# Expert layers: the clamp of a block's last two hidden chunks, moved from VectorE to GpSimd

## What is computed

```python
def _expert(x, g, b, W1, b1, W2, b2, Wo, bo):
    x = _layernorm(x, g, b)
    x1 = x @ W1 + b1
    x2 = jnp.clip(x @ W2 + b2, -20.0, 20.0)
    hidden = jnp.clip(x1 * (x2 * jax.nn.sigmoid(x2)), -10000.0, 10000.0)
    return jnp.clip(hidden @ Wo + bo, -10000.0, 10000.0)
...
logits = xf @ router_w
scores, idx = jax.lax.top_k(logits, 2)
gate = jax.nn.softmax(scores, axis=-1)
```

## Time and profile before

| | |
|---|---|
| median of 3 runs | 2541.86 us (2539.79 to 2549.73) |
| profiled execution, its own time | 2537.98 us |
| its span, first to last instruction | 2536.1 us |
| first expert pass, first to last `product` | 280.5 to 485.3 us |
| second expert pass, first to last `product` | 2296.7 to 2505.5 us |
| busy over the span: PE, DVE, ACT, POOL | 2306.2, 2218.5, 1652.6, 1483.1 us |
| back clamp L1791 on DVE, both passes | 80 times, 32.8 us |
| front clamp L1741 on POOL, both passes | 80 times, 44.9 us |
| scatter L1732 on POOL, both passes | 142 times, 143.2 us |

### The profile page before, as it was taken

How to read it: one execution, slowest core, us unless ns; L and a number is a source line. 1 busy time by engine, 2 the same in 40 slices (tenths; PEclk the granted TensorE clock), 3 DMA queues, 4 the chain that set the end, 5 groups by cost and what they waited for, 6 DMA issues and landing times. The chain is left out here.

```text
span 2536.1 us, 44098 instructions
## 1 busy us (share of the span) xinstructions
PE 2306.2 (91%) x14954; PEld 1766.5 (70%) x14954; DVE 2218.5 (87%) x4734; ACT 1652.6 (65%) x2883; POOL 1483.1 (58%) x1075
## 2 busy tenths in 40 slices
PE   6996699658999999999999999999999999968995
PEld 3553588536777777777777777777777777747884
DVE  6766588779999999999999999999999999956886
ACT  2464244347777777787778778788778877743443
POOL 1145344326666666667668766676876766663442
PEclk8997799869999999999999999999999999988997
DMA  8821566654534454344322333223342233006665
GB/s 206 221 64 46 161 210 215 174 132 108 126 84 97 98 128 99 84 101 110 84 62 71 87 81 88 62 62 79 86 100 62 62 79 86 15 27 196 202 212 180
DMA packets 169648, 281.89 MB, mean 111 GB/s; under 512 B 32940, under 2 KB 122930, under 8 KB 169424
## 3 DMA queue, kind: packets, MB, share of 16 engines
q1 hardware_dynamic: 160208, 260.11, 40.6%
q0 software_dynamic: 9216, 18.96, 2.1%
HBM read 118.94 MB, written 62.39 MB: 72 GB/s over the span
## 5 line engine op out<-in xcount | busy, mean ns | idle before, releaser
L2438 POOL TENSOR_TENSOR b_prob<-b_prob,b_weight 128x1024 f32<-128x1024 f32 x512 | 958.7, 1905 | 505.5 <-DVE b_weight L2396 504.3
L2366 DVE TENSOR_REDUCE b_bmax<-b_score 128x16 f32<-128x1024 f32 x512 | 620.5, 1212 | 44.8 <-PE b_score L2217 29.3
L2318 ACT ACTIVATE b_prob<-b_score,b_neg_m 128x1024 f32<-128x1024 f32 x512 | 581.4, 1136 | 76.9 <-DVE b_neg_m L2374 75.1
L2353 DVE TENSOR_REDUCE b_bsum<-b_prob 128x16 f32<-128x1024 f32 x512 | 605.5, 1202 | 0.0
L2303 ACT ACTIVATE b_pT<-b_turn 128x512 f32<-128x512 f32 x1024 | 560.4, 609 | 63.4 <-PE b_turn L2230 55.2
L2230 PE MATMUL b_turn<-ident,b_prob 128*128 128x128 f32 x4096 | 532.1, 273 | 3.7 <-ACT b_pT L2303 3.6
L2230 PEld LDWEIGHTS b_turn<-ident,b_prob 128*128 128x128 f32 x4096 | 477.7, 140 | 75.7 <-ACT b_pT L2303 3.9
L2217 PE MATMUL b_score<-b_KH,b_QS 128*128 128x512 f32 x1024 | 478.8, 468 | 16.8 <-ACT b_prob L2318 14.6
L2197 PE MATMUL b_acc<-b_pT,b_V 128*64 128x256 f32 x4096 | 470.3, 382 | 0.0
L2217 PE MATMUL b_score<-b_KL,b_QS 128*128 128x512 f32 x1024 | 405.6, 396 | 0.0
L2197 PEld LDWEIGHTS b_acc<-b_pT,b_V 128*64 128x64 f32 x4096 | 282.7, 137 | 150.7 <-issue 21.4
(11 more groups left out here) (329 smaller groups left out, 2956.6 us busy)
## 6 DMA issues: line engine op xcount, KB each, us to landing
f_e_w<-f_weights SPq DMA_DIRECT2D x80, 776.0 KB
f_sorted<-zeros SPq DMA_DIRECT2D x172, 193.5 KB, 5.4
b_KH<-b_k_high SPq DMA_DIRECT2D x128, 256.0 KB
b_KL<-b_k_low SPq DMA_DIRECT2D x128, 256.0 KB
b_QS<-b_q_high SPq DMA_DIRECT2D x64, 256.0 KB, 3.8
b_QS<-b_q_low SPq DMA_DIRECT2D x64, 256.0 KB, 4.9
b_hb<-b_hT SPq DMA_DIRECT2D x31, 512.0 KB
f_e_z<-f_sorted SPq DMA_DIRECT2D x62, 129.0 KB
```

What stands on the lines that cost most here:

```text
L2318: act.activation(prob[r % 4][k][:], score[k % 2][:], ACT.Exp, bias=neg_m[r % 2][:, k:k + 1]).then_inc(prob_ready, 1)
L2353: dve.tensor_reduce(bsum[r % 2][:, k, :], prob[r % 4][k][:].rearrange("p (n c) -> p n c", c=KV_BLOCK), AX, ALU.add).then_inc(sum_ready, 1)
L2366: maxima = chain.mark(dve.tensor_reduce(bmax[r % 2][:, k, :], score[k % 2][:].rearrange("p (n c) -> p n c", c=KV_BLOCK), AX, ALU.max))
L2438: pool.tensor_tensor(tile, tile, weight[r % 2][:, k, :].unsqueeze(2).to_broadcast([P, NB, KV_BLOCK]), ALU.mult).then_inc(scaled, 1)
```

## The change

GpSimd makes the clamp of chunks 2 and 3, behind its store of block t - 2, after a wait for all four products of block t. VectorE's `clamp_back` goes, with its two waits. Since another engine now reads `hid[1]`, VectorE waits for `back_ready` of block t - 1 before product 2 of block t. What is clamped, and the semaphore that tells it, stay the same.

```diff
@@ gpsimd @@
                     if t >= 2:
                         store(t - 2)
+                    pool.wait_ge(x1_taken, chunks_before + HC * t + HC)
+                    pool.tensor_scalar(hT[t % DEEP][:, 2:HC, 0:rows_of[t]], hid[1][:, :, 0:rows_of[t]], CLAMP, -CLAMP, ALU.min, ALU.max).then_inc(back_ready, 1)
@@ vector, product @@
                     if c == 0 and t >= 1:
                         dve.wait_ge(front_ready, blocks_before + t)
+                    if c == 2 and t >= 1:
+                        dve.wait_ge(back_ready, blocks_before + t)
...
-                def clamp_back(t, i):
-
-                    dve.wait_ge(x1_taken, chunks_before + HC * t + HC)
-                    if t >= DEEP:
-                        dve.wait_ge(down_done, blocks_before + t - DEEP + 1)
-                    dve.tensor_scalar(hT[i][:, 2:HC, 0:rows_of[t]], hid[1][:, :, 0:rows_of[t]], CLAMP, -CLAMP, ALU.min, ALU.max).then_inc(back_ready, 1)
@@ vector, step @@
-                        if c == HC - 1:
-                            clamp_back(t, i)
```

## The result

| | before | after |
|---|---|---|
| median of 20 runs each | 2542.07 us (2535.69 to 2549.73) | 2547.53 us (2543.30 to 2552.72) |
| ratio to the kernel before | | 1.0025, 95% interval 1.0017 to 1.0032 |
| span of the profiled execution | 2536.1 us | 2549.9 us |
| first front clamp to last scatter's end, both passes added | 420.1 us | 426.4 us |

The account below looks back on a forecast made before the run. TensorE was taken to bound both expert passes, with VectorE in slack. Kind A +1.9, kind B +1.5 and the pass ends +0.8 summed to +4.2 us, giving a forecast of 2546 us, range 2536 to 2556.

Parts of the forecast that it names:

- TensorE sets the pace: Both expert passes: TensorE bounds, VectorE has 31 to 34 us slack per pass; removing its 32.8 us of clamps alone gains nothing.
- GpSimd's path: From the front clamp's start, through two scatters, to a second clamp usable by the down product: 3.88 us.
- Kind A: Full block with a small one behind it: down load 0.12 us later in each of 16 blocks, +1.9 us.
- Kind B: Full block behind a small one: down loads late in 10 blocks, 1.2 to 2.2 us in all, taken as +1.5.
- block D: Full block behind a Kind B block: only one scatter ahead of its clamp, so more room and no cost forecast.
- Kind C: Full block between full blocks: need of 4.24 us against a path of 3.88 us, so no cost.
- End of a pass: Last block's second clamp goes between the scatters of blocks 37 and 38: +0.4 us, twice, +0.8 us.
- The new wait at product 2: VectorE waits there for the previous block's second clamp: no cost, over 1 us of room; rival that it stalls, chance 0.02.
- The port: VectorE's output clamp and GpSimd's new clamp exclude each other: VectorE waits up to 0.4 us in A, GpSimd 0.14 in B.
- Faster: Rival: second clamp never late at down, so 0.36 us gained in each of 16 Kind A blocks; 2536 us, chance 0.12.
- Slower: Rival: GpSimd later still at down, from a longer scatter gap and the output clamp; 2553 to 2558 us, chance 0.20.
- transfers hide things: Rival: where rows `z` come late, a later down costs nothing; +2 us or less, 2544 us, chance 0.12.

## Why the prediction held, step by step

- **TensorE sets the pace, VectorE's relief by itself is worth little.** Right: leaving the clamp out altogether gave 0.9992. The sign that I gave for it was off in size: VectorE's idle time ahead of its clips was to rise by some 15 us a pass, and its wait for TensorE rose by 6.8 and 2.1, because ScalarE's activations took as much of the freed time.
- **GpSimd's path, 3.88 us.** It measured 3.80 (3.79 to 3.82) in 16 of the 18 A blocks and 7 of the 16 B blocks; in the others the load came later, 3.91 to 5.83 us after the front clamp. With early rows it is 3.79 to 3.81 in 33 of the 34. Two terms were off and partly cancel: the gap behind the scatter, 0.13 taken, is 0.01 (373.86 + 0.98 = 374.84, clamp at 374.85), and the clamp lasts 0.65 us there, not 0.61. The release is 0.07.
- **Kind A, +0.12 us each.** The load-to-load time rose by 0.11. Right, and so was the reason: what up product 3 gains is lost at down. That the number fits so well is luck in part: the path is 0.08 shorter than forecast, and against the down load ahead of it the front clamp starts only 0.10 earlier, not 0.17. The whole stake, 0.36 forecast, is 0.37 when the clamp goes between the scatters (4.92 to 4.55).
- **Kind B, 1.5 us in all.** There are 16 such blocks, not 10, once transfers don't delay them, each 0.21 late; but block D gives 0.15 back. Net 0.06 each, about 1.0 us. The size came out near for two omissions of opposite sign.
- **Kind C free.** Right.
- **End of a pass, +0.4 each.** 0.37 and 0.36.
- **The new wait at product 2.** No row of the waits shows VectorE waiting for GpSimd. Right.
- **The sum, +4.2.** 5.5 measured, 4.4 without waits for `z`; the 1.1 us between them are within the noise of the two. TensorE's waits for `z` are 6.7 and 8.4 us in the changed kernel's windows, 3.0 and 8.4 before; whether the change causes that is open, as the waits vary from run to run.
- **The port.** The Trainium skill (SBUF — State Buffer, Who interferes with whom) has the second comer wait for the whole instruction of the first. The trace agrees: the output clamp takes 0.54 us in kind A and 0.63 in B where it took 0.29 and 0.23, and ends 0.16 and 0.08 us after GpSimd's clamp. In kind B I had VectorE first; it was GpSimd, 385.02 before 385.13, as the gap behind the scatter is zero. Of the 30 times that the two clamps meet in the changed kernel, GpSimd was first in 29; the one time that VectorE was, by 0.02 us, GpSimd's clamp took 0.68 us. So GpSimd lost next to nothing, and VectorE's slack took the rest. Nor did the scatters get shorter without L1791 beside them: 0.98 us at 373.86, as at 441.38.
- **The rivals.** Faster needed a path about 0.5 us shorter, which the clamp between the scatters has (it ends 2.80 us after the front clamp's start); there it pays 4 us and not the 5.8 I gave. Slower, +11 us and more, didn't come: it needed GpSimd to come second at the port and a gap of 0.30. That transfers hide things was true, but for the gain rather than for the loss.

## What to carry to other kernels

When work moves to an engine with slack, ask where in that engine's queue it lands: here 2.3 us of scatters stood ahead of a 0.6 us clamp on which the bounding engine waits, and one scatter's difference turned 4 us of loss into 4 us of gain. Read the need in the tightest kind of block, not in the average one. If an expected gain doesn't show, look for a transfer that was just in time before: only with the rows requested early did the freed time count, and that reordering by itself gave more (8 us) than the whole change could. The fastest kernel here is the clamp between the scatters with early rows, at 0.9947 of the kernel before.

## Of the hardware, not expected

- A compute instruction on GpSimd can start 0.01 us after a scatter ends, where two scatters are 0.31 us apart. It then lasts 0.65 us against 0.60 when it has waited for its input.
- VectorE's output clamp is also held up by a scatter. In the three kernels with the back clamp ahead of or between the scatters, where it starts 0.55 to 0.7 us after a scatter it takes 0.44 to 0.52 us instead of 0.29 (256 elements) or 0.23 (128) and ends 0.04 to 0.13 us after the scatter. In the kernel before, with and without early rows, where L1791 started 0.39 to 0.49 us after a scatter, it kept its 0.43 or 0.29 us.
- The waits for `z` are probably a part of the run-to-run spread. The kernel before has a standard deviation of 3.8 us on the second chip (20 runs) and 2.8 on the third (13 runs); the six kernels with early rows have 1.2 to 2.7 (5 to 10 runs each), which is too few to say how much. The chips themselves differ by some 10 us (2542.07 and 2530.61 to 2532.16).
